# Batch 0's head stores are waited for in the second attention; five low parts move to GpSimd; low and middle parts go ahead of the next pair

## The reference

```python
x = x + _L0_ffn_ref(_layernorm(x), gate_w, w1, w2, w3)
x = x + _L1_attn_ref(_layernorm(x), W_qkv, b_qkv, W_out, b_out, rel_emb_k, rel_emb_v)
# in _L1_attn_ref, 16 heads of 16 values:
qkv = (x @ W_qkv + b_qkv).reshape(b, s, 3, H, hd)
score = einsum('bhqd,bhkd->bhqk', q, k) + einsum('bhqd,qkd->bhqk', q, pe_k)   # pe_k from rel_emb_k by distance
ctx = einsum('bhqk,bhkd->bhqd', softmax(score), v) + einsum('bhqk,qkd->bhqd', softmax(score), pe_v)
```

## Time and profile before

| | us |
|---|---|
| median of three runs | 1758.69 |
| profiled execution | 1761.55 |
| its span, first to last instruction | 1759.8 |
| busy in the span: TensorE / DVE / ACT / GpSimd | 1564.3 / 1014.5 / 887.0 / 563.5 |

### The profile page before, as it was taken

The page is one execution under the profiler, slowest core; times in us unless marked ns, Lnnn a source line. Parts: engine busy times, 40 slices in busy tenths (PEclk is TensorE's granted clock), DMA queues, the critical chain, the costliest instruction groups (busy, mean ns, idle before and its releaser), DMA issues. The chain is left out here.

```text
span 1759.8 us, 34234 instructions
## 1 busy us (share of the span) xinstructions
PE 1564.3 (89%) x12792; PEld 1071.0 (61%) x12792; DVE 1014.5 (58%) x2073; ACT 887.0 (50%) x1480; POOL 563.5 (32%) x817
## 2 busy tenths in 40 slices
PE   7689989878479999999975899999999999997988
PEld 3333333256368766776753577777777777775544
DVE  6577777335332111111166888888788888873566
ACT  5256656732331111111134788888788888873321
POOL 4311111122313000000253355555555565542111
PEclk9799999987779999999997899999999999998899
DMA  5811111030123133221237797886868778544101
GB/s 161 235 25 24 24 27 21 1 132 19 42 75 132 63 120 128 87 87 60 61 96 187 214 224 203 199 212 195 208 191 201 201 201 210 172 133 172 49 12 36
DMA packets 209796, 213.06 MB, mean 121 GB/s; under 512 B 19651, under 2 KB 187217, under 8 KB 209505
## 3 DMA queue, kind: packets, MB, share of 16 engines
q1 hardware_dynamic: 199969, 192.52, 40.3%
q0 software_dynamic: 4864, 13.64, 2.3%
q10 hardware_dynamic: 4800, 4.72, 0.8%
HBM read 128.82 MB, written 81.81 MB: 120 GB/s over the span
## 5 line engine op out<-in xcount | busy, mean ns | idle before, releaser
L1353 DVE CUSTOM_DVE_ANT_0 prob<-ps,dev 128x1024 f32<-128x1024 f32 x256 | 311.6, 1218 | 3.0 <-DMA skew_p<-prob 2.9
L1246 ACT ACTIVATE prob<-prob,nmax 128x1024 f32<-128x1024 f32 x256 | 293.2, 1146 | 7.5 <-DVE nmax L1353 7.3
L1162 PE MATMUL ps<-cst,prob 128*128 128x128 f32 x2048 | 278.8, 277 | 0.1
L2048 PE MATMUL ps<-xeT,w 128*128 128x384 f32 (+2 forms) x896 | 256.3, 448 | 5.1 <-DVE hT L2252 4.4
L1162 PEld LDWEIGHTS ps<-cst,prob 128*128 128x128 f32 x2048 | 227.7, 141 | 42.3 <-issue 21.0
L1381 DVE COPY probT<-ps 128x512 f32<-128x512 f32 x256 | 176.4, 689 | 101.5 <-PE ps L1162 101.5
L868 ACT ACTIVATE pT<-ps 128x512 f32<-128x512 f32 (+3 forms) x384 | 166.1, 495 | 118.3 <-PE ps L824 115.9
L906 DVE TENSOR_REDUCE nmax<-ps 128x1 f32<-128x128 f32 (+7 forms) x256 | 184.0, 753 | 70.7 <-PE ps L803 69.5
L2048 PEld LDWEIGHTS ps<-xeT,w 128*128 128x128 f32 x896 | 177.0, 198 | 77.8 <-DVE hT L2252 4.8
L2112 ACT ACTIVATE xT_c<-ps 128x256 f32<-128x256 f32 (+2 forms) x98 | 46.6, 476 | 326.3 <-PE ps L2048 326.2
L1255 ACT ACTIVATE probT<-ps 128x512 f32<-128x512 f32 x256 | 151.3, 591 | 101.2 <-PE ps L1162 101.0
(11 more groups left out here) (322 smaller groups left out, 2284.5 us busy)
## 6 DMA issues: line engine op xcount, KB each, us to landing
dev<-skew_u SPq DMA_DIRECT2D x128, 256.0 KB, 3.5
skew_p<-prob SPq DMA_DIRECT2D x128, 256.0 KB, 3.4
w<-in_L_ffn_w SPq DMA_DIRECT2D x20, 896.0 KB, 6.3
skew_u<-cst SPq DMA_DIRECT2D x64, 256.0 KB, 4.0
pre<-skew_p SPq DMA_DIRECT2D x128, 128.0 KB, 2.9
qs<-qd SPq DMA_DIRECT2D x72, 128.0 KB, 3.8
vz<-in_L_ffn_w SPq DMA_DIRECT2D x10, 896.0 KB, 5.6
ks1firsta<-kd SPq DMA_DIRECT2D x24, 256.0 KB, 5.7
```

Source lines behind the costliest of these rows:

```text
L1162: last = nc.tensor.transpose(ps[:, ring_bank(job), kb * P:(kb + 1) * P], prob_tile(t, (4 * h + kb) * P, (4 * h + kb + 1) * P), k.c("ident"))
L1246: nc.scalar.activation(prob_tile(t, 0, S), prob_tile(t, 0, S), ACT.Exp, bias=nmax[:, t % 4:t % 4 + 1], scale=-1.0).then_inc(s_exp, 1)
L1353: nc.vector.tensor_tensor_reduce(out=prob_tile(t, 0, S), in0=scores, in1=dev_tile(t), scale=-1.0, scalar=3.0e38, op0=ALU.add, op1=ALU.min, ...
L2048: last = nc.tensor.matmul(ps[:, a + z * wide + h, 0:cols], w[:, j, c, f * P:(f + 1) * P], xeT[:, c, h * cols:(h + 1) * cols], start=(c == ...
```

## The change

In the expert stage, SP no longer waits for all stores at the end; GpSimd does the lows of pairs 5 to 7 (units 7 to 11) behind its gathers, and `low` takes the engine as an argument and waits for the low before it; SP loads the first queries behind store 6 and not behind store 8; ACT does the middles of pair 7 ahead of `normed(3)`. The semaphores of the head stores are no longer in the list that is cleared at the end of a stage. In `attention1`, the wait for batch 0's stores stands in SP's step 1 and on DVE behind step 8, ahead of the memsets of `prob`, which move there from the start. In step n ACT does middles of n - 1, highs of n, stores of n - 1; DVE does lows of n - 1, then residues and values of n.

```diff
@@ Heads.__init__
-        self.s_st = [k.sem(f"s_h{b}st{n}") for n in range(deep)]
+        self.s_st = [k.nc.alloc_semaphore(name=f"s_h{b}st{n}") for n in range(deep)]
@@ Heads
-    def low(self, dve, i):
-        nc = self.k.nc
-        dve.wait_ge(self.s_mid, i + 1)
-        dve.wait_ge(self.s_res, i + 1)
-        nc.vector.tensor_tensor(self.parts[:, i % self.deep, 2, :], self.res[:, i % self.RES, :], self.parts[:, i % self.deep, 1, :],
+    def low(self, eng, i):
+        eng.wait_ge(self.s_mid, i + 1)
+        eng.wait_ge(self.s_res, i + 1)
+        if i:
+            eng.wait_ge(self.s_lo, i)
+        eng.tensor_tensor(self.parts[:, i % self.deep, 2, :], self.res[:, i % self.RES, :], self.parts[:, i % self.deep, 1, :],
                                 ALU.subtract).then_inc(self.s_lo, 1)
@@ attention1, SP, step of the loop
+                        if n == 1 and step % 16 == 1:
+                            k.heads0.stored(sp)
@@ attention1, ACT, step ("project", n)
+                        if n:
+                            for i in proj.of(n - 1):
+                                proj.middle(act, i)
                         if n < len(proj.prods):
                             for i in proj.of(n):
                                 proj.high(act, i)
                         if n:
-                            for i in proj.of(n - 1):
-                                proj.middle(act, i)
-                        if n > 1:
-                            for i in proj.of(n - 2):
-                                proj.store(act, i)
-                        if n == len(proj.prods):
                             for i in proj.of(n - 1):
                                 proj.store(act, i)
@@ attention1, DVE, start
-                nc.vector.memset(prob[:, 0:SLOTS * PITCH].rearrange("p (s w) -> p s w", w=PITCH)[:, :, 0:PAD], 0.0)
-                nc.vector.memset(prob[:, SLOTS * PITCH:SLOTS * PITCH + PAD], 0.0)
@@ attention1, DVE, step ("project", n)
+                        if n:
+                            for i in proj.of(n - 1):
+                                proj.low(dve, i)
                         if n < len(proj.prods):
                             for i in proj.of(n):
                                 proj.residue(dve, i)
                             proj.values(dve, n)
-                        if n:
-                            for i in proj.of(n - 1):
-                                proj.low(dve, i)
                         if n == len(proj.prods):
                             dve.wait_ge(proj.s_v, KB)
                             nc.vector.memset(ps[:, 7, :], 0.0).then_inc(s_clear, 1)
+                            k.heads0.stored(dve)
+                            nc.vector.memset(prob[:, 0:SLOTS * PITCH].rearrange("p (s w) -> p s w", w=PITCH)[:, :, 0:PAD], 0.0)
+                            nc.vector.memset(prob[:, SLOTS * PITCH:SLOTS * PITCH + PAD], 0.0)
@@ experts
-            proj = Heads(k, over, 0, 6, None, (6, 7))
+            proj = k.heads0 = Heads(k, over, 0, 6, None, (6, 7))
@@ experts, SP
                 for i in range(len(proj.units)):
                     proj.store(sp, i)
-                    if i == 8:
+                    if i == 6:
                         proj.stored(sp, 6)
                         for c in range(TERMS):
                             load_part(sp, k, c, 0, q0, k0, k.s_q0, k.s_k0)
                 for c in range(TERMS, 2 * TERMS):
                     load_part(sp, k, c, 0, q0, k0, k.s_q0, k.s_k0)
-                proj.stored(sp)
@@ experts, ACT
                 rooted(3)
+                middles(KB - 1)
                 normed(3)
-                middles(KB - 1)
                 turned(3)
@@ experts, GpSimd
                 gather(1, len(items) - 1)
+                for n in range(5, KB):
+                    for i in proj.of(n):
+                        proj.low(pool, i)
@@ experts, DVE
                 summed(3)
-                lows(5)
                 residues(7)
                 shifted(3)
-                lows(6)
-                lows(7)
```

## The result

The changed kernel takes 1755.16 us, the median of 20 runs (1751.81 to 1758.27), against 1758.9 for the kernel before, 20 runs taken beside it (1755.56 to 1764.07). The ratio is 0.9978, 95% interval 0.9970 to 0.9986: 3.9 us faster, between 2.5 and 5.3. The forecast was 8.4 us faster, 1750.3. The sign and the two places were right, the size was not.

What follows compares the result with a forecast made beforehand. The seam was taken as bound by DMA landings and behind them one serial chain, no engine full. Seam 6.1 (6.5 - 0.35) plus front 2.3 gave 8.4 us: 1758.7 to 1750.3 us, range 1747.0 to 1754.3.

Steps and rivals of the forecast that it cites:

- step 1: End of expert stage: SP leaves once its last K load is issued, not after store landings; alone 3.9 us.
- step 2: Expert stage: shorter chain of residues, middles, lows, stores and loads; SP done at 945.0 against 951.5, 6.5 us with step 1.
- the first rival: GpSimd's drain tail follows its last work, barrier waits until 949.1: seam gives 2.0, time 1754.3 us; chance 0.09.
- GpSimd beside DVE: Expert stage: GpSimd's lows hold up DVE's two gather additions; cost 0.8 us, from nothing to 2.4.
- step 3: Semaphore clearing: six fewer cleared may split one range clear in two; cost 0.35 us, bounds 0 and 0.6.
- step 4: Front of second attention: earlier stores free slots, ACT's 6.5 us of waits go; gain 2.3 us, bounds 0.2 to 3.4.
- the ring of two pairs: Front: chain residue, middle, high, residue sets the pace, 5.3 us per two pairs, against TensorE's 5.15.
- The 0.6 for slowed lows: Front: 0.6 us added because DVE's lows run slower beside GpSimd's work.
- the 0.6 for ACT's issues: Front: 3 x 0.2 us added for ACT issuing two stores where the next middle is ready sooner.
- the clock: Rival: a shorter pause before the second attention keeps TensorE's clock up, first pair 2.5 us faster, 1747.8 us; chance 0.11.
- SP could issue ahead: Rival denied this: K loads' issuing waits for earlier loads, SP done near 949 to 951, about 1756 us; chance 0.05.
- GpSimd's lows were not slow: Rival claimed the five serial lows become the chain, kernel slower; 4.1 us per low would give 1762.2; chance 0.04.

Runs made afterwards that it cites:

- e3: Changed kernel plus a drain instruction on GpSimd between its last gather and its first low; 1748.53 us, run once.
- e10: Changed kernel plus a GpSimd drain right behind the gathers of batch 0, with 18 more GpSimd DMAs after it; 1749.94 us, run once.
- e4: Changed kernel with each low's added wait for the low before it kept only for unit 7 of batch 0; 1752.81 us, ratio 0.9977 to before.
- e12: e3 with e4's edit, prob's memsets in step 3 on DVE, and six K loads right behind the Q loads; 1753.66 us, ratio 0.9963 to before.
- e6: e3 with the six K loads moved from the end of the expert stage to SP's start in attention1; 1750.63 us, ratio 0.9960 to before.
- e8: e6 with e4's edit, and batch 1's stores in the front issued by SP, not ACT; 1753.17 us, ratio 0.9970 to before.
- e9: Kernel before plus 24 small GpSimd DMAs through the second attention, each waited for at once; 1823.46 us, run once.

## Why the prediction was wrong

- **The waits leave the block** (step 1): right. SP passed no wait for head stores, and those that were added in attention1 took no time.
- **The chain before SP's last issue** (step 2): its length was right, 12.2 against 12.3 us, and its role was not. This is the step that failed: "SP is done at 945.0. [...] Against 951.5 this is 6.5 us" takes for granted that SP is the last at the barrier. The seam gave 2.1. The barrier waited for GpSimd's drain, 7.94 us past the last low, which is the first rival: it gave 2.0 for the seam, 1754.3 in all, and got a chance of 0.09. What spoke against it, that compute on GpSimd started without idle time behind 16 indirect DMAs, was read wrongly: a later instruction doesn't pay, only a drain does (e3). The row that decided was at hand, the drain of 15.94 us, of which 7.9 lay past the last gather; the change put work behind the gathers and so carried that tail, whole, to the end of the block. With the tail paid earlier the seam is 14.16 (e3) and 13.95 (e10), against the 14.3 forecast.
- **GpSimd beside DVE**: 0.8 forecast, 0.96 measured (2.02 against 1.06). Singly the additions took 0.70 and 1.22 where they take 0.48 alone. The exclusive lock of the Trainium skill (SBUF — State Buffer, section "SBUF: two separate sides") is borne out in that both were held; but they began when 0.43 and 0.93 us of a low were left and lost 0.22 and 0.73, so the loss was less than what was left of it, and the 1.6 us more that I gave as the rule's price did not come. The low that was to start at once waited 0.17 us each time for the one before: 1.32 from start to start, not 1.22.
- **Clearing** (step 3): two range clears, 68 and 505 ns, and one drain more, in all about 0.1 us longer against 0.35.
- **The front** (step 4): 1.77 against 2.3, and that it came so near is luck: 0.73 of the 1.77 lie ahead of the residues of pair 1, where TensorE's clock came back sooner, which no term of the step had. The step's own terms gave 1.03. The waits for stores went, as said. Residues of pair 1 to pair 7 took 17.98 and not 17.1, since the ring of two pairs is 5.68 and not 5.3. 0.22 of it is the added wait in `low`, which the step never priced (e4). The rest is a wait that it placed wrongly: in e4's clean round the next residue, at 974.52, follows DVE's two lows, while the high it needs ended at 974.31; so with the odd pair DVE's lows end last, and not middle and high. The 0.6 for slowed lows came as 0.66, the 0.6 for ACT's issues as 0.27. And the residue of pair 7 to the maximum got 0.16 longer, where 0.2 was to be gained: one low less gives 0.6, but the memsets of prob cost 0.53 on the path and the added wait 0.22.
- **The other rivals**: the clock did not come back for the first product (0.50 until 952.8); it came back sooner for the second, with the 0.73 us above in place of the 2.5 of the rival. SP could issue ahead here; in e12, with the key loads ahead too, it could not. GpSimd's lows were not slow.

The two misses add up: 4.0 us in the seam and 0.5 in the front (1.3 short in its terms, 0.7 back by the clock) are the 4.5 between the forecast 8.4 and the 3.9 of the lengths.

## What to carry to other kernels

Where an engine's last work of a block is moved, read what its drain did before, and ask what the drain will end behind now: a long drain in the shade is a price that moves with the last instruction. On GpSimd count the DMAs since its last drain; if work is to stand behind many of them, put a drain ahead of that work, in a time in which GpSimd waits anyway. And a transfer that is moved out of a barrier's way must be followed to where it lands: e6 gave back in the front, waiting for a store's landing, what it had won in the seam, and in e12 the issue of the stores became slow.

## What the runs showed of the hardware that was not expected

- A drain on GpSimd lasts about 0.08 us longer for each DMA that GpSimd has issued since its last drain. Added were 0.10 for one and 1.97 for 24; past the last instruction it ended 1.55 for 18, 6.44 for 78 and 7.9 for 96, and 0.07 for none.
- The issue of one DMA from SP, 0.36 to 0.6 us as a rule, took 3.66 and 3.25 us behind 16 others of 128 to 384 KB (e12), and one from ACT took 0.88 (the kernel after) and 1.42 (e4) in place of 0.37. That the DMAs in flight are the cause was not tried by itself, and one of 1.25 us came in e6 with only three issued in the 6 us before.
- A wait on DVE for the instruction just before it costs 0.22 us (1.50 against 1.28 for two lows, of which the second waits), on GpSimd 0.2 (lows 1.32 apart, and 1.12 in e8, where five without the wait took 5.61).
- The stretch from the first maximum to the end, the same code in all these kernels, took from 769.7 to 775.1 us in one profiled execution each (e9, which changes that stretch, left out). This is why single times can't place a gain of 2 us, and lengths of a stretch can. Its cause stays open.
